# Loading the edge lists as rows of 1024, and normalising with two engines, ahead of a two-layer graph kernel

## The reference

```
h1  = segment_sum(w[:, None] * (layernorm(x) @ W1)[src], dst) + b1
z   = leaky(concat(h1, layernorm(x)[root]))
h2  = segment_sum(w[:, None] * (z @ W2)[src], dst) + b2
x1  = x + leaky(concat(leaky(h2), h1[root]) @ Wl + bl)
r   = layernorm(x1) @ wr + br                  # one router weight per node
sel = the 3124 nodes with the largest r
out = x1 + layernorm(x1);  out[sel] += r[sel] * (gelu(layernorm(x1)[sel] @ w1 + b1') @ w2 + b2')
```

## Time and profile before

| what | us |
|---|---|
| median of 3 runs (lowest, highest) | 2211.76 (2207.11, 2212.53) |
| the profiled execution | 2209.72 |
| its span, first to last instruction | 2207.7 |
| PE busy | 1693.9 (77%) |
| POOL busy | 1511.5 (68%) |
| DVE busy | 1149.4 (52%) |
| ACT busy | 371.0 (17%) |

### The profile page before, as it was taken

One profiled execution on the slowest core, in us unless ns is written; L12 is line 12 of the kernel. 1 busy time (PEld: TensorE's weight loads), 2 busy tenths in 40 slices (PEclk: granted clock), 3 DMA queues, 4 the chain that ended last, 5 costly groups with the idle time before them and its releaser, 6 DMA issues.

```text
span 2207.7 us, 39619 instructions
## 1 busy us (share of the span) xinstructions
PE 1693.9 (77%) x7203; PEld 1361.6 (62%) x7204; DVE 1149.4 (52%) x4020; ACT 371.0 (17%) x938; POOL 1511.5 (68%) x1588
## 2 busy tenths in 40 slices
PE   0277777777767766767679999989998999988881
PEld 0165556555545554555468888878777777777660
DVE  5654445444444343333356666666565555555446
ACT  2300000000000000000112222222222222222230
POOL 1377777777777777777577777777777777777500
PEclk9998899888888888887899999999999999999995
DMA  6633333333333333333233333333333333333203
GB/s 193 183 111 109 110 111 109 109 112 111 108 112 112 111 109 110 112 110 109 81 106 104 103 104 102 103 104 105 104 103 104 105 104 103 103 104 105 76 0 116
DMA packets 109339, 236.70 MB, mean 107 GB/s; under 512 B 28862, under 2 KB 58683, under 8 KB 109310
## 3 DMA queue, kind: packets, MB, share of 16 engines
q0 software_dynamic: 75392, 205.62, 31.9%
q1 hardware_dynamic: 19048, 19.22, 2.7%
q10 hardware_dynamic: 14870, 11.58, 1.6%
HBM read 216.94 MB, written 19.38 MB: 107 GB/s over the span
## 4 chain that ended last, share of the span: by engine, by line
POOL 44%; PE 25%; issue 18%; DVE 5%; DMA 4%; DVEq 2%; ACTq 1%; ACT 0%; POOLq 0%
POOL ring L283 44%; PE ps_agg L489 13%; PE ps_dn L583 4%; PE ps_up L590 4%; DMA ring<-conv_rows,idx 2%; DMA ring<-normed_rows,idx 2%; DVE S L768 1%; ACTq L305 1%; DVE xs L990 1%; PE ps_dn L581 1%; PE ps_o L553 1%; PE ps_o L621 1%; DMA acc<-in_dst 1%; DVE acc L776 0%; DVE ring L699 0%
## 5 line engine op out<-in xcount | busy, mean ns | idle before, releaser
L489 PE MATMUL ps_agg<-ring,S 128*128 x3136 | 869.7, 426 | 342.7 <-DMA ring<-normed_rows,idx 162.1
L489 PEld LDWEIGHTS ps_agg<-ring,S 128*128 128x128 f32 x3136 | 643.7, 212 | 511.0 <-issue 416.6
L283 POOL DMA_INDIRECT ring<-normed_rows,idx x784 | 752.0, 959 | 282.8 <-issue 234.1
L283 POOL DMA_INDIRECT ring<-conv_rows,idx x784 | 752.9, 960 | 256.2 <-issue 231.6
L776 DVE TENSOR_TENSOR acc<-acc,ps_agg x490 | 206.5, 421 | 651.3 <-PE ps_agg L489 601.1
L768 DVE TENSOR_SCALAR S<-iota,dstc,wc 128x128 f32<-128x128 int16 x1584 | 448.5, 363 | 153.9 <-issue 124.2
L489 PE MATMUL ps_agg<-ring,S_more 128*128 x768 | 192.2, 395 | 19.8 <-DVE S_more L768 18.1
L583 PE MATMUL ps_dn<-fw2s,hT 128*128 128x256 f32 x864 | 206.2, 393 | 0.0
L590 PE MATMUL ps_up<-xnT,fw1s 128*128 128x256 f32 x832 | 190.5, 382 | 1.2 <-ACT hT L400 1.2
L583 PEld LDWEIGHTS ps_dn<-fw2s,hT 128*128 128x128 f32 x864 | 163.4, 194 | 39.6 <-issue 18.6
L489 PEld LDWEIGHTS ps_agg<-ring,S_more 128*128 128x128 f32 x768 | 150.5, 199 | 54.0 <-issue 32.1
(11 more groups left out here) (175 smaller groups left out, 981.9 us busy)
## 6 DMA issues: line engine op xcount, KB each, us to landing
ring<-normed_rows,idx POOLq DMA_INDIRECT x784
ring<-conv_rows,idx POOLq DMA_INDIRECT x784
conv_rows<-rows ACTq DMA_DIRECT2D x50, 128.0 KB
out_rows<-xs SPq DMA_DIRECT2D x6, 896.0 KB
xs<-in_x SPq DMA_DIRECT2D x4, 1280.0 KB, 14.3
normed_rows<-acc SPq DMA_DIRECT2D x4, 1280.0 KB, 5.2
normed_rows<-acc SPq DMA_DIRECT2D x1, 1152.0 KB, 4.8
xs<-in_x SPq DMA_DIRECT2D x1, 1024.0 KB
```

The costliest lines, as they stand in the source:

```text
L283: pool.indirect_dma_start(out=ring[:, slot * TG + t, :], out_offset=None, in_=f_dram if l == 0 else t2_dram, in_offset=bass.IndirectOffset ...
L489: last = nc.tensor.matmul(to, select[:, t, :], moving, start=(t == 0), stop=(t == TG - 1))
```

## The change

The edge lists are loaded as 98 rows of 1024 edges (CH is 8 pieces of 128 now, where it was 7; a row holds the edges of eight tiles, that is of two groups): 96 rows by one transfer, the 97th by another and the 672 edges of the 98th by a third. The second copy of `dst` is gone, and the reductions over groups read the floated rows. POOL's conversion of `src` also clamps it. ACT takes the turned lists out of PSUM, and puts the columns back into the order of the tiles. DVE computes the statistics of all chunks before it reduces over groups and makes the tables. The chunks of x go from the last node down, and the window of 106 rows is loaded as SP's second transfer. Of each chunk POOL normalises the last three windows and ACT the rest. The clearing of `acc` is moved: POOL clears a chunk once the chunk is stored, ACT the last one, DVE only the four slots below the windows, at the start. The two tiles without an edge are no longer gathered, in either layer; their place in the ring is cleared once. The core of the diff:

```diff
-    CH = 7
+    CH = 2 * TG
...
+    SPARE = NT - -(-E // P)
...
-        XCH = [(0, 10), (10, 20), (20, 30), (30, 40), (40, NW)]
+        XCH = [(40, NW), (30, 40), (20, 30), (10, 20), (0, 10)]
...
             for c, (w0, w1) in enumerate(XCH):
                 wf = min(w1, NW - 1)
                 sp.dma_start(xs[:, X0 + w0:X0 + wf, :], x[w0 * P:wf * P, :].rearrange("(w p) d -> p w d", p=P)).then_inc(x_loaded[c], 16)
-            sp.wait_ge(xs_cleared, 1)
-            sp.dma_start(xs[0:LAST_ROWS, X0 + NW - 1, :], x[(NW - 1) * P:N, :]).then_inc(x_loaded[-1], 16)
+                if w1 == NW:
+                    sp.wait_ge(xs_cleared, 1)
+                    sp.dma_start(xs[0:LAST_ROWS, X0 + NW - 1, :], x[(NW - 1) * P:N, :]).then_inc(x_loaded[c], 16)
             for c, (w0, w1) in enumerate(XCH):
                 sp.wait_ge(f_ready, c + 1)
-                sp.dma_start(f_dram[w0 * P:w1 * P, :].rearrange("(w p) d -> p w d", p=P), f_rows[:, w0:w1, :]).then_inc(f_stored, 16)
+                sp.wait_ge(f_ready_pool, c + 1)
+                sp.dma_start(f_dram[w0 * P:w1 * P, :].rearrange("(w p) d -> p w d", p=P), f_rows[:, w0:w1, :]).then_inc(f_stored[c], 16)
...
-            nc.gpsimd.memset(src_rows[:, CH - 1, :], 0).then_inc(edges_cleared, 1)
-            nc.gpsimd.memset(dst_rows[:, CH - 1, :], N - 1).then_inc(edges_cleared, 1)
-            nc.gpsimd.memset(w_rows[:, CH - 1, :], 0.0).then_inc(edges_cleared, 1)
-            nc.gpsimd.memset(dst_groups[:, 1, :], N - 1).then_inc(edges_cleared, 1)
+            link(nc.gpsimd.memset(ident[:, :], 0.0))
+            nc.gpsimd.affine_select(out=ident[:, :], in_=ident[:, :], compare_op=ALU.not_equal, fill=1.0, base=0,
+                                    pattern=[[-1, P]], channel_multiplier=1).then_inc(consts_ready, 1)
+            nc.gpsimd.memset(spare_rows, 0.0)
+            nc.gpsimd.iota(iota[:, :], pattern=[[1, 2 * P]], base=0, channel_multiplier=0).then_inc(iota_ready, 1)
+
+            pool.wait_ge(src_loaded, 16 * 3)
+            nc.gpsimd.tensor_scalar(src_rowsf, src_rows, 0.0, float(N - 1), ALU.max, ALU.min).then_inc(rows_floated, 1)
+            pool.wait_ge(dst_loaded, 16 * 3)
+            nc.gpsimd.tensor_copy(dst_rowsf, dst_rows).then_inc(rows_floated, 1)
             pool.wait_ge(xs_cleared, 1)
             for q in range(QG):
                 part = slice(q * D // QG, (q + 1) * D // QG)
                 pool.dma_start(fb2r[:, part], fb2[part].rearrange("(o n) -> o n", o=1)).then_inc(landed[1][q], 16)
-            link(nc.gpsimd.memset(ident[:, :], 0.0))
-            nc.gpsimd.affine_select(out=ident[:, :], in_=ident[:, :], compare_op=ALU.not_equal, fill=1.0, base=0,
-                                    pattern=[[-1, P]], channel_multiplier=1).then_inc(consts_ready, 1)
-
-            pool.wait_ge(edges_loaded, 16 * 9)
-            nc.gpsimd.tensor_copy(src_rowsf[:, :, :], src_rows[:, :, :]).then_inc(rows_floated, 1)
-            nc.gpsimd.tensor_copy(dst_rowsf[:, :, :], dst_rows[:, :, :]).then_inc(rows_floated, 1)
-            nc.gpsimd.iota(iota[:, :], pattern=[[1, 2 * P]], base=0, channel_multiplier=0).then_inc(iota_ready, 1)
+            for c, (w0, w1) in enumerate(XCH):
+                pool.wait_ge(stats_ready, c + 1)
+                for w in range(w1 - BY_POOL, w1):
+                    last = nc.gpsimd.tensor_scalar(f_rows[:, w, :], xs[:, X0 + w, :], rstd[:, w:w + 1], nmr[:, w:w + 1], ALU.mult, ALU.add)
+                last.then_inc(f_ready_pool, 1)
+                if c > 0:
+                    w0, w1 = XCH[c - 1]
+                    pool.wait_ge(f_stored[c - 1], 16)
+                    nc.gpsimd.memset(acc[:, A0 + w0:A0 + w1, :], 0.0).then_inc(cleared, 1)
...
                 if l == 0:
-                    pool.wait_ge(f_stored, 16 * len(XCH))
+                    pool.wait_ge(diag_ready, 1)
+                    pool.wait_ge(f_stored[-1], 16)
                 else:
                     pool.wait_ge(t2_stored, 16 * (NW + 2))
...
                         tile = (NIT - 1 - it) * RING + q * TG + t
+                        if tile >= NT - SPARE:
+                            continue
                         pool.indirect_dma_start(out=ring[:, slot * TG + t, :], out_offset=None, in_=f_dram if l == 0 else t2_dram,
                                                 in_offset=bass.IndirectOffsetOnAxis(ap=idx[:, tile:tile + 1], axis=0)).then_inc(landed[slot // QG][q], 16)
...
+            act.wait_ge(edges_cleared, 1)
+            for a, r, loaded in ((src, src_rows, src_loaded), (dst, dst_rows, dst_loaded), (edge_weight, w_rows, w_loaded)):
+                act.dma_start(r[0:96, :], a[0:full].rearrange("(r e) -> r e", e=EW)).then_inc(loaded, 16)
+                act.dma_start(r[96:97, :], a[full:more].rearrange("(r e) -> r e", e=EW)).then_inc(loaded, 16)
+                act.dma_start(r[97:98, 0:E - more], a[more:E].rearrange("(r e) -> r e", r=1)).then_inc(loaded, 16)
...
+            for i, (banks, to) in enumerate(zip(turned, columns)):
+                act.wait_ge(edges_turned, i + 1)
+                for h, bank in enumerate(banks):
+                    last = nc.scalar.activation(to.rearrange(by_chunk, c=CH)[:, h * TG:(h + 1) * TG, :], bank[:, 0:TG * CR].rearrange("p (c r) -> p c r", c=TG), ACT.Copy)
+                last.then_inc(edges_kept, 1)
+
             for c, (w0, w1) in enumerate(XCH):
                 act.wait_ge(stats_ready, c + 1)
-                for w in range(w0, w1):
+                for w in range(w0, w1 - BY_POOL):
                     last = nc.scalar.activation(f_rows[:, w, :], xs[:, X0 + w, :], ACT.Identity, scale=rstd[:, w:w + 1], bias=nmr[:, w:w + 1])
                 last.then_inc(f_ready, 1)
-            act.wait_ge(f_stored, 16 * len(XCH))
+            for stored in f_stored:
+                act.wait_ge(stored, 16)
+            w0, w1 = XCH[-1]
+            nc.scalar.activation(acc[:, A0 + w0:A0 + w1, :], zeros[:, 0:1].unsqueeze(2).to_broadcast([P, w1 - w0, D]), ACT.Copy).then_inc(cleared, 1)
...
-            nc.scalar.activation(acc[:, ZCUT:NACC, :], zeros[:, 0:1].unsqueeze(2).to_broadcast([P, NACC - ZCUT, D]), ACT.Copy).then_inc(cleared, 1)
...
-            for r, (b0, b1_) in zip((src_rowsf, dst_rowsf, w_rows), banks):
+            for i, (r, (b0, b1_)) in enumerate(zip((src_rowsf, dst_rowsf, w_rows), banks)):
+                if i < 2:
+                    pe.wait_ge(rows_floated, i + 1)
+                else:
+                    pe.wait_ge(w_loaded, 16 * 3)
                 for c in range(CH):
-                    to = b0[:, c * CR:(c + 1) * CR] if c < 4 else b1_[:, (c - 4) * CR:(c - 3) * CR]
-                    last = nc.tensor.transpose(to, r[:, c, :], ident[0:CR, 0:CR])
+                    to = (b0, b1_)[c // TG][:, (c % TG) * CR:(c % TG + 1) * CR]
+                    last = nc.tensor.transpose(to, r[:, c * P:(c + 1) * P], ident[0:CR, 0:CR])
                 last.then_inc(edges_turned, 1)
...
-                pe.wait_ge(landed[0][q], (it >> 1) * LAND + (1 + (NIT + 1) // 2 * l) * LAND)
+                short = 16 * SPARE * (l + 1) if q == QG - 1 else 0
+                pe.wait_ge(landed[0][q], (it >> 1) * LAND + ((1 + (NIT + 1) // 2 * l) * LAND - short))
                 pe.wait_ge(landed[1][q], ((it + 1) >> 1) * LAND + (16 + NIT // 2 * l * LAND))
...
-            V.memset(acc[:, DUMMY + 1:A0 - 1, :], 0.0)
+            tail = E - (CR - 1) * EW
+            V.memset(src_rows[96:CR, tail:EW], 0)
+            V.memset(dst_rows[96:CR, tail:EW], N - 1)
+            V.memset(w_rows[96:CR, tail:EW], 0.0).then_inc(edges_cleared, 1)
+            V.memset(acc[:, 0:A0, :], 0.0).then_inc(cleared, 1)
             V.memset(xs[:, 0:X0, :], 0.0)
             V.memset(xs[:, X0 + NW - 1:NX, :], 0.0).then_inc(xs_cleared, 1)
...
-            normalise((0, 1))
-
-            dve.wait_ge(groups_loaded, 16 * 3)
-            link(V.tensor_reduce(nmax[0:GR, 0, :], dst_groups[:, :, :], AX.X, ALU.min))
-            link(V.tensor_reduce(nmax[0:GR, 1, :], dst_groups[:, :, :], AX.X, ALU.max))
+            normalise(range(len(XCH)))
+
+            dve.wait_ge(rows_floated, 2)
+            by_group = dst_rowsf.rearrange("p (c e) -> p c e", c=2)
+            link(V.tensor_reduce(nmax[0:GR, 0, :], by_group, AX.X, ALU.min))
+            link(V.tensor_reduce(nmax[0:GR, 1, :], by_group, AX.X, ALU.max))
...
             last.then_inc(diag_ready, 1)
-
-            normalise((2,))
-
-            dve.wait_ge(edges_turned, 3)
-            c4 = 4 * CR
-            for b, n, m in ((ps_t, 0, c4), (ps_h, c4, NT)):
-                last = V.tensor_scalar(idx[:, n:m], b[:, 0:m - n], 0.0, float(N - 1), ALU.max, ALU.min)
-            last.then_inc(edges_kept, 1)
-            V.tensor_copy(dstc[:, PADT:PADT + c4], ps_o[:, 0:c4])
-            V.tensor_copy(dstc[:, PADT + c4:PADT + NT], ps_dn[:, 0:NT - c4]).then_inc(edges_kept, 1)
-            V.tensor_copy(wc[:, PADT:PADT + c4], up_flat[:, 0:c4])
```

(8 more changed lines are left out.)

47 lines of the change are left out of this document (18 added, 29 removed).

## The result

| | before | after |
|---|---|---|
| median, us (lowest, highest; runs) | 2209.6 (2207.11, 2212.53; 4) | 2173.18 (2169.19, 2178.37; 4) |
| profiled execution (its span) | 2209.72 (2207.7) | 2178.37 (2176.6) |
| ratio of the times | | 0.9836 [0.9809, 0.9863] |

The change takes 36.2 us (30 to 42) off by the ratio, and 36.4 by the two medians; the forecast was 29.9. The time of 2173.18 lies just outside the range of 2174 to 2189.

A forecast was written before the change was run, and what follows sets the result against it. POOL's gather pace was taken to bound both layers, after a late first gather. Prologue 24.8 plus left-out gathers 5.1 made 29.9 off the profiled 2209.72, so 2179.8, or 2181.9 by the median; forecast 2181 us, range 2174 to 2189.

The forecast's parts named there:

- What sets the end: Whole kernel: POOL's pace sets both layers, so only an earlier first gather and fewer gathers can pay.
- The gathers: Both layers: two of 784 gathers left out in each, worth 1.264 us apiece, 5.1 us in all.
- two layers of gathers, plus parts that stay: Whole time: first gather at 81.68 us, then both layers at 1.264 us a gather, then parts the change leaves alone.
- DVE's start: Prologue: DVE begins the first chunk at 12.3 us, between 10.3 and 14.4, where it was 8.78 before.
- The second rival: Prologue: the 106-row window lands slowly, DVE starts at 18, everything is 6 us later, 2187; chance 0.1.
- Statistics: Prologue on DVE: one chunk of 6.67 us and four of 7.06 follow without a wait, ending at 47.2.
- The first rival: Prologue: POOL and DVE block each other, statistics up to 14 us later, 2195; chance 0.12 of over 6 us.
- The last chunk: End of prologue: ACT's seven windows 3.5 us, POOL's 0.5 each, then 6.1 to the first gather at 56.9.
- Lists, tables and the start of PE: Prologue and early layer 1: this work stays under cover; tables end by about 57, `diag_ready` comes at 51.
- Between the layers: From layer 1's last gather to layer 2's first: 17.54 us before, about 17 expected, not touched by the change.
- The sum: Whole kernel: 24.8 us from the prologue plus 5.1 from left-out gathers make 29.9 less; forecast 2181 us.

The follow-up runs named there:

- a_all2: The changed kernel with all 784 gathers in each layer, on a chip where the kernel before takes 2210.97 us: 2177.32 us, ratio 0.9851 [0.9835, 0.9868].

## Why the prediction was wrong

Its account of where the time goes held; two sizes did not, and they erred in opposite directions.

**What sets the end.** Right: both layers go at POOL's pace, and an earlier first gather and fewer gathers were paid in full.

**The failed step** is "**The gathers**" together with the sentence on which it stands, that the time is first gather, "two layers of gathers, plus parts that stay". It priced the gathers that went (5.1, measured 5.3) and took the other 1564 to cost 1.264 each, as before, without a range for it. They cost 1.260 in the changed kernel's profiled execution (6.8 us) and 1.258 in `a_all2` (10.5 us for 1566 steps of 0.0067). A difference of 0.5% in an instruction seemed nothing; multiplied by the number of times that POOL does it, it is larger than the whole gain from leaving gathers out.

**DVE's start.** Predicted 12.3 between the bounds 10.3 and 14.4; measured 14.84, 2.5 late and above the upper bound. The bound came so close by luck, since both of its terms were off: the issue of the window took 0.32 us and not 4.83, and the statistics started 9.9 behind it and not 5.2.

```profile
4.61 0.32 SPq L237 DMA_DIRECT2D xs<-in_x  x1
```

The 5.2 is the landing of a store. The prediction calls the stores SP's only landing rows, but the profile before had one for the loads of x themselves, and with 14.3 in place of 5.2 the bound would have lain well above 14.84:

```profile
xs<-in_x SPq DMA_DIRECT2D x4, 1280.0 KB, 14.3
```

The second rival, a late first chunk, came true at less than half its size (2.5 of 6 us). Every pair of kernels here speaks for cutting at 96 rows (list pieces: a wait of 21 us gone; the window: 2.3 us). The rule that the prediction cites from the Trainium skill (DMA: Bandwidth & Descriptors, Why a DMA increments its semaphore by 16 and not by 1) points the same way, but the estimate of about 12 made with it did not hold, and even after the cut 2.07 of the wait stay.

**Statistics.** 7.06 a chunk was right except for the one operation under POOL's clear: 1.6 us. The first rival thus had a true core, far smaller than its 14 us, while POOL's work on windows and DVE's statistics did not lengthen each other. The rule it cited from the Trainium skill (SBUF — State Buffer, SBUF: two separate sides) agrees in kind: a small operation of the Newton steps waited behind a clear, and statistics did not. Its estimate of 4 to 8 us in all was too high: only one of the clears that met DVE's work lay on the path.

**The last chunk.** 0.55 for a window of POOL (0.5 taken), 3.55 for ACT's seven (3.5), 6.1 from ACT's end to the first gather (6.1). The first gather at 60.97 and not 56.9 is DVE's start (2.5) plus the clear (1.6). Gain 20.7 instead of 24.8.

**The rest.** Lists, tables and the start of PE stayed under cover, the tables with less to spare than predicted: POOL's conversion of `src` took 3.64 us where about 1.07 was put, `diag_ready` came at about 56.6 and not 51, and the tables ended at 63.8 and not 57, still ahead of DVE's first `S` at 73.3. Between the layers, predicted as unchanged: 1.6 us more in this execution, but 2.2 less in `a_all2` (1061.9 - 1045.6 = 16.3). Two variants of the kernel before on that chip show 16.2 and 17.5, where the first profile of before had 18.5, so this part moves by some 2 us without the change.

**The sum.** Forecast 24.8 + 5.1. Measured by the profiled spans: 20.7 + 5.1 + 6.8 - 1.6 + 0.1 = 31.1, which would have been inside the range. The median is 5.2 below that execution. `a_all2`, whose four runs lie within 4 us, shows what a usual run is made of: 21.0 for the prologue, 10.5 for shorter gathers, 2.2 between the layers, less 1.6 behind them, 32.1 in all; with 5.1 for the left-out gathers 37.2, against the 36.4 between the medians. Another 2.2 of the miss is that the median of before came out at 2209.6 when its kernel ran once more beside the changed one.

**What stays open** is why the gathers are shorter. Long (953) are those of the kernel before and of it with five more semaphores, without two gathers, or with cut pieces. Short (946 to 949) are those of all nine variants of the changed kernel, and of the kernel before with one clamp or with two tiny operations on POOL. Excluded by the runs: the number and order of the semaphores, the left-out gathers, the order of the chunks, the clamp, POOL's windows and its clears, each by a kernel that lacks it and is short, or has it and is long. The number of POOL's instructions ahead of the gathers does not sort them either: the kernel with the clamp has as many as before and is short, the one without two gathers has one more and is long. What all short kernels share, as far as the runs go, is only that POOL's program ahead of the gathers differs from that of before in its arithmetic instructions; leaving gathers out brought a clear of the ring with it there, and that one alone did not do it.

## What to carry to other kernels

When one short instruction, repeated over a thousand times, sets the pace, treat its duration as a term with its own uncertainty: 7 ns of 953 were worth 10 us here. Look at the row counts of the transfers before rearranging a prologue: cutting pieces of 97 to 109 rows at 96 brought the first gather forward by 20.4 us, where the whole rearrangement with all its gathers gave 21.0, and a window of 106 rows moved to the front took part of the rest back. Large clears on POOL belong beside work of DVE that they do not hold up, or on ACT.

## What the runs showed of the hardware

- Chips differ: the same program took 2210 us where it was first timed and on one more chip, and 2727 to 2757 on four others. There single instructions of DVE wait up to 9.4 us, in one run 18.9, with nothing recorded that releases them (at most 1.7 in any profile on the other two), and POOL idles 510 to 563 us for places in its ring. The mean granted clock of TensorE in the profiled runs was 0.82 to 0.85 there and 0.90 to 0.92 where the kernel before takes 2210. Which of these is cause and which consequence, and whether it is the chip or something else that ran beside, no run tells. Fewer gathers are worth nothing there (the left-out gathers: 0.9993 [0.9968, 1.0018]).
- POOL's clamp of 98x1024 from int32 to f32 took 3.64 us and the CAST of the same size 1.04, while a window of 128x256, also two arithmetic steps but from f32, took 0.55. That is 3.6 and 2.1 ns an element of a row.
- An f32 operation of 128x10 on DVE waited for the end of a clear on POOL (1.77, 2.20, 1.26 us instead of 0.17, each ending with the clear); statistics did not.
